# A graph network on one core: the two convolution passes take one-hots from memory and run their maxima on 32 rows, and the gated pass makes its angle on TensorE

## The chip, the cores and the metric

One core of a Trainium2 chip runs the whole program in one launch. The metric is the device time of that core in microseconds (us). Five engines take part: TensorE (PE; its weight loads are PEld), VectorE (DVE), ScalarE (ACT), GpSimd (POOL) and SyncE (SP), each with a sequencer of its own that issues its instructions in program order, waits for semaphores and does register work.

## The reference

Four graph layers run over 6,250 nodes with 128 features and 100,000 edges, each followed by a residual sum and a layer norm. The last layer is two transformer convolutions that share their edge features:

```python
    # L1: a gate per edge
    edge_weights = sigmoid(relu(ef @ We1 + be1) @ We2 + be2)[:, 0]
    aggr = segment_sum(edge_weights[:, None] * h_src, col, num_segments=n)
    # L3
    rel_t = last_update[src] - t
    rel_t_enc = jnp.cos(rel_t[:, None] * Wt[0][None, :] + bt)
    edge_attr = jnp.concatenate([rel_t_enc, msg], axis=-1)
    def transformer_conv(x, src, dst, edge_attr, ...):        # called twice, 4 heads of 32
        e = (edge_attr @ We).reshape(-1, HEADS, C)
        k_j = k[src] + e
        v_j = v[src] + e
        alpha = einsum('ehc,ehc->eh', q[dst], k_j) / sqrt(C)
        amax = segment_max(alpha, dst, num_segments=n)
        expa = exp(alpha - amax[dst])
        denom = segment_sum(expa, dst, num_segments=n)
        out = segment_sum(expa / denom[dst] * v_j, dst, num_segments=n)
        return out + x @ Wskip + bskip
```

## The kernel before

The edges are sorted by destination into 110 superblocks (turns) of 1,024 slots: eight tiles of 128 edges, in four groups of two tiles, each group with destinations of one bin of 128 nodes. A pass over the edges is a software pipeline of turns. There are seven: three relational attention passes, the gated pass (`gated_edges`), the attention pass of L2, and two convolution passes (`attention_edges` with `conv=1` and `conv=2`). The prediction speaks of the gated pass and of the two convolution passes.

The order on every engine is written out by hand in a function `step`. In a convolution pass `superblocks` calls it with three turns at once: `n` is scored, `m` gets its maxima and weights, `o` is summed. What happens to a turn:

- POOL gathers its 1,024 source rows with eight indirect DMAs (L970) into one of four buffers; it may start when the sums of the turn four back are done.
- DVE builds its one-hot, 128x1024, destination place by edge (`make_onehot`, L946). TensorE transposes it (L1087) and ACT copies it (L1203).
- TensorE spreads q of the destination with the flipped one-hot (L1109) and multiplies the edge features with We (L1112), in two halves of four tiles through one PSUM bank (`spread_half`). DVE adds e to k and v and multiplies with q (`convolve_half`, L1249 to L1251) and reduces to four scores per edge (`make_score`, L1288).
- Eight transposes bring the scores to 4 rows of 1,024 (`turn_scores`, L1122). Two scans of DVE run along them, up (L1258) and down (L1265), and give every edge the maximum of its segment, with the last turn's end carried in. Eight small transposes turn them back (`turn_top`, L1133), with the fall of the running maximum (L1272, L1135).
- DVE subtracts (L1279), ACT makes rate, factor and the exponentials (L1208, L1210, L1214), DVE weighs the rows (L1304), TensorE sums two tiles at a time with the one-hot (`sum_group`, L1147), and DVE adds each group's sum to its bin (`add_sums`, L1314).

Which bin a group has is read at run time: `load_bin` (L936) reads one number from SBUF into a register of the engine that asks, by the sequencer. TensorE and DVE read four a turn, ACT one. In `step` of DVE they stand in pairs behind the two scans; TensorE has its four between the third sum and the first half.

The gated pass works on turns `n` and `o`: one-hot, flip (L1452), copy (L1505), spread (L1467), dot product with the gate's weights (L1590 to L1597), sigmoid (L1517), weighing (L1545), sums (L1489, L1538). Beside it DVE makes the angle `rel*Wt+bt`, and takes whole turns off (L1561 to L1586, seven instructions, behind L1559 that makes `rel`); ACT takes the cosine (L1510), TensorE flips the features (L1478), ACT copies them (L1514), and SP stores them to DRAM (`edge_feat`) for the convolutions. DVE's four bin loads stand one by one between the instructions of the angle.

## Time and profile before

| what | us |
|---|---|
| median of 3 runs | 15725.96 (15695.67 to 15761.44) |
| profiled execution: span from first to last instruction | 13400.0 |
| gated pass, in the span | 6573 to 7999 |
| L2's attention pass | 8356 to 9512 |
| first convolution pass | 9796 to 11474 |
| second convolution pass | 11613 to 13303 |

The profiled execution's own time is not given beside its span. The timed runs are 2,326 us longer than the span, and no row shows what lies in that difference. Over the span DVE is busy for 78%, PE for 64%, POOL for 52% and ACT for 27%. A pass is read as 110 turns: a turn's time is the distance between two occurrences of an instruction that stands in it once.

### The profile page before, as it was taken

The page shows a single profiled execution, that of the slowest core. Times are in us where ns is not written, and L with a number is a line of the kernel's source. Part 1 is how long each engine was busy: PE and PEld are TensorE (multiplying, and loading weights), DVE is VectorE, ACT ScalarE, POOL GpSimd, SP SyncE. Part 2 cuts the span into 40 slices and gives each one's busy share as a digit, 9 for nine tenths or more (in the row PEclk, how much of TensorE's full clock was granted, in tenths as well). Part 3 has the DMA queues.
Part 4 walks back from the last instruction along what each step waited for, and adds up shares of the span by engine and source line. Part 5 has one row for each costly group of instructions (what it writes and reads, how often), then busy time and mean ns, then how long its engine had stood idle before and what let it go on. Part 6 is the DMA issues. An engine that isn't in the chain of part 4 may idle for free. (4 is left out here: it accounts for less than half of the span.)

```text
span 13400.0 us, 212567 instructions
## 1 busy us (share of the span) xinstructions
PE 8527.8 (64%) x52858; PEld 6962.8 (52%) x52859; DVE 10400.3 (78%) x15015; ACT 3614.6 (27%) x7819; POOL 6926.8 (52%) x7047
## 2 busy tenths in 40 slices
PE   4663477776777677775465652777266666567764
PEld 3553245554455535654455542555266666566664
DVE  8666569974799748996688875888778888688888
ACT  0111133332333233332244431333211111111111
POOL 2775047750477407772277750777145555255553
PEclk8555688877888788887688875666588888788887
DMA  4334754444544474443255550222233334233333
GB/s 182 113 113 119 244 206 106 106 80 193 192 106 106 72 292 123 106 106 53 79 145 145 146 111 19 55 55 54 19 103 106 107 107 105 75 108 105 105 106 72
DMA packets 720185, 1523.62 MB, mean 114 GB/s; under 512 B 364796, under 2 KB 416585, under 8 KB 680627
## 3 DMA queue, kind: packets, MB, share of 16 engines
q0 software_dynamic: 306624, 795.04, 25.0%
q1 hardware_dynamic: 413427, 727.07, 15.9%
q8 instruction: 51, 0.84, 0.0%
q14 instruction: 83, 0.68, 0.0%
HBM read 1050.48 MB, written 471.10 MB: 114 GB/s over the span
## 5 line engine op out<-in xcount | busy, mean ns | idle before, releaser
L970 POOL DMA_INDIRECT h<-table,edges_ring x3984 | 3856.5, 968 | 1889.0 <-issue 1154.3
L1147 PE MATMUL bank<-h,edges_onehot 128*128 128x260 f32 (+1 forms) x7968 | 1986.6, 406 | 652.3 <-issue 469.0
L1147 PEld LDWEIGHTS bank<-h,edges_onehot 128*128 128x128 f32 x7968 | 1570.6, 246 | 978.1 <-issue 717.4
L970 POOL DMA_INDIRECT edges_rows<-table,edges_ring x1512 | 1527.0, 1010 | 716.0 <-issue 431.0
L1122 PE MATMUL bank<-ident,edges_score 128*4 128x128 f32 x5280 | 1027.7, 360 | 1021.5 <-DVE edges_score L1288 737.9
L1258 DVE TENSOR_TENSOR_SCAN bank<-edges_fresh,edges_top,bank 4x1024 f32<-4x1024 bf16 x660 | 1541.5, 2336 | 144.9 <-PE bank L1122 141.2
L1265 DVE TENSOR_TENSOR_SCAN edges_top<-edges_fresh,bank 4x1024 f32<-4x1024 bf16 x660 | 1493.8, 2263 | 0.6 <-issue 0.3
L1122 PEld LDWEIGHTS bank<-ident,edges_score 128*4 128x4 f32 x5280 | 497.6, 104 | 1339.0 <-DVE edges_score L1288 784.9
L1314 DVE TENSOR_TENSOR acc<-acc,bank 128x260 f32 (+1 forms) x2640 | 908.9, 344 | 164.4 <-PE bank L1147 60.4
L2017 POOL DMA_INDIRECT rec<-dst,slots x782 | 797.0, 1019 | 432.7 <-issue 432.4
L1203 ACT ACTIVATE edges_onehotT<-bank 128x1024 bf16<-128x1024 bf16 (+1 forms) x550 | 562.1, 1022 | 1153.3 <-PE bank L1087 715.9
L970 POOL DMA_INDIRECT acc<-table,edges_ring x664 | 722.1, 1088 | 265.9 <-issue 199.8
L959 POOL COPY edges_ring<-rel_idx 128x64 uint32 (+2 forms) x42 | 10.3, 246 | 1575.5 <-POOLq L150 1575.4
L1191 ACT ACTIVATE edges_narrow_onehot<-edges_onehot 128x1024 bf16<-128x1024 f32 x444 | 469.2, 1057 | 1088.4 <-DVE edges_onehot L946 1088.4
L959 POOL COPY edges_ring<-src_idx 128x64 uint32 (+2 forms) x56 | 13.4, 239 | 1435.9 <-POOLq L150 1324.7
L1147 PE MATMUL bank<-edges_rows,edges_onehot 128*128 128x260 f32 (+1 forms) x2592 | 638.2, 401 | 169.3 <-issue 132.8
L1112 PE MATMUL bank<-edges_w_e,edge_score 128*128 128x128 f32 x3520 | 707.7, 284 | 0.0
L1208 ACT ACTIVATE edges_rate<-bank 128x4 f32<-128x4 f32 x660 | 114.4, 173 | 2168.8 <-PE bank L1135 2164.6
L1185 ACT ACTIVATE acc<-acc,edges_factor x2640 | 627.3, 309 | 92.3 <-issue 91.4
L1147 PEld LDWEIGHTS bank<-edges_rows,edges_onehot 128*128 128x128 f32 x2592 | 500.6, 240 | 281.4 <-issue 150.6
L1304 DVE TENSOR_TENSOR h<-h,bank 128x1024 f32<-128x1024 f32 x498 | 605.7, 1216 | 3.2 <-ACT bank L1214 1.1
L354 PE MATMUL bank<-source_w_rel,source_curT 128*128 128x512 f32 x1176 | 549.3, 612 | 88.5 <-DVE x L420 33.3
(346 smaller groups left out, 18152.3 us busy)
## 6 DMA issues: line engine op xcount, KB each, us to landing
table<-x SPq DMA_DIRECT2D x154, 1040.0 KB, 7.9
edge_score<-edge_feat SPq DMA_DIRECT2D x220, 512.0 KB, 3.8
table<-h SPq DMA_DIRECT2D x77, 1040.0 KB, 7.9
table<-source_typed_rows SPq DMA_DIRECT2D x63, 1040.0 KB, 8.1
h<-table,edges_ring POOLq DMA_INDIRECT x3984
edge_feat<-edge_score SPq DMA_DIRECT2D x110, 512.0 KB, 2.9
dst_row<-dst_rows SPq DMA_DIRECT2D x71, 704.0 KB, 4.2
buf<-rec SPq DMA_DIRECT2D x44, 840.0 KB, 5.2
```

What stands on the lines that cost most here:

```text
L354: ins = pe.matmul(g.bank[2 + half][:, q * 512:(q + 1) * 512], curT[:, j, :], w_rel[:, r:r + 4, :].rearrange("p r c -> p (r c)"), start=Tru ...
L970: pool.indirect_dma_start(out=rows[s % R][:, j, :], out_offset=None, in_=table, in_offset=bass.IndirectOffsetOnAxis(ap=ring[:, s * ST + j: ...
L1112: ins = pe.matmul(flip_b[:, 512 + j * P:512 + (j + 1) * P], feat[:, s, tile * P:(tile + 1) * P], w_e[:, :], start=True, stop=True)
L1122: ins = pe.transpose(score_b[0:HEADS, j * P:(j + 1) * P], score[s][:, j, :], g.ident[:, :])
L1147: ins = pe.matmul(sum_b[k % 3], onehot[s][:, j, :], rows[s][:, j, A0:W], start=j == k * GT, stop=j == (k + 1) * GT - 1)
L1185: ins = act.activation(part, part, ACT.Copy, scale=factor[s][:, head:head + 1])
L1203: act.activation(flippedT[s][:, :, :].rearrange("p t c -> p (t c)"), narrow_b[:, :] if conv is None else flip_b[:, :], ACT.Copy).then_inc( ...
L1258: v.tensor_tensor_scan(score_b[0:HEADS, :], fresh[s][:, 0:SLOTS_SB], score_b[0:HEADS, :], top[1 - s][:, SLOTS_SB - 1:SLOTS_SB], ALU.add, A ...
L1265: v.tensor_tensor_scan(top[s][:, ::-1], fresh[s][:, SLOTS_SB:0:-1], score_b[0:HEADS, ::-1], -BIG, ALU.add, ALU.max).then_inc(top_made, 1)
L1304: v.tensor_tensor(zr, zr, weight_t.unsqueeze(3).to_broadcast([P, ST, HEADS, DH]), ALU.mult).then_inc(rows_weighted, 1)
L1314: v.tensor_tensor(part, part, sum_b[k % 3], ALU.add).then_inc(sums_taken, 1)
L2017: pool.indirect_dma_start(out=rec, out_offset=bass.IndirectOffsetOnAxis(ap=slots[s][0:n, j:j + 1], axis=0), in_=recs[s][0:n, j * REC:(j + ...
```

## The change

**Convolution passes.** A new function `conv_edges` takes the place of `attention_edges` for them.
- One-hot and flipped one-hot are no longer made: SP loads both, 512 KB each a turn, from DRAM, where the gated pass has stored them.
- The pipeline has four stages (`stages`, turns `p, n, m, o`): the halves of turn `p` are spread one turn before DVE takes them, and each half has a bank of its own.
- The scores are kept as 32 rows (head by tile) of 128. One transpose turns them. The maxima have two levels: `find_ends` reduces each row's open ends (two instructions, each with a second that writes the 32x1 result), `line_up` brings these 64 numbers into one row on TensorE, `link` scans them (two scans of 32), `turn_line` turns them back, and `scan_both` runs two scans of 32x128 from there. The marks for it (`marks_d`, `lines_d`) are made once, before the passes.
- DVE's four bin loads stand together at the start of `step`, TensorE's between the second sum and `turn_line`. Sums are awaited in pairs.

**Gated pass.** The angle is one transpose of `rel` (9x128) and one product of 9x128 with a 9x512 table; DVE rounds it and subtracts (two instructions for seven). The flip of the one-hot runs a turn ahead, after the angle, and SP stores one-hot and flipped one-hot. The bin loads of DVE and of TensorE stand four in a row.

```diff
+def conv_edges(g, name, conv):
+                def load_features(p):
+                    hold(sp, half_ready, 2 * (u - 1))
+                    sp.dma_start(feat[s], g.edge_feat[:, bass.ds(u * (ST * P), ST * P)]).then_inc(feat_in[s], 16)
+                    sp.dma_start(onehotT[s], g.flip_d[:, bass.ds(u * (ST * P), ST * P)]).then_inc(feat_in[s], 16)
...
+                def step(p, n, m, o):          # TensorE
+                    if m:
+                        line_up(m)
+                    if o:
+                        sum_group(o, 0)
+                        sum_group(o, 1)
+                    if p:
+                        bins = load_bins(pe, g, number(p))
+                    if m:
+                        turn_line(m)
+                    if p:
+                        spread_half(p, 0, bins)
+                    if o:
+                        sum_group(o, 2)
+                        sum_group(o, 3)
+                    if m:
+                        turn_top(m)
+                    if p:
+                        spread_half(p, 1, bins)
+                    if n:
+                        turn_scores(n)
...
+                    act.activation(drop[:, :], drop_b, ACT.Relu).then_inc(drop_taken, 1)
+                    act.wait_ge(drop_taken, u + 1)
+                    act.activation(rate[s % 2][:, :], drop[:, :], ACT.Exp, scale=-1.0).then_inc(rate_made, 1)
...
+                def step(p, n, m, o):          # DVE
+                    bins = load_bins(v, g, number(o)) if o else []
+                    if m:
+                        find_ends(m)
+                    if n:
+                        convolve_half(n, 0)
+                    if o:
+                        add_sums(o, 0, bins)
+                        add_sums(o, 1, bins)
+                    if m:
+                        link(m)
+                    if n:
+                        convolve_half(n, 1)
+                    if m:
+                        scan_both(m)
+                    if n:
+                        make_score(n)
+                    if o:
+                        add_sums(o, 2, bins)
+                    if m:
+                        subtract_top(m)
+                    if o:
+                        add_sums(o, 3, bins)
+                    if m:
+                        weigh_rows(m)
...
+                def step(n, o, more=True):     # gated pass, TensorE
+                    if n:
+                        spread(n, load_bins(pe, g, number(n)))
+                    if o:
+                        sum_group(o, 0)
+                        sum_group(o, 1)
+                    if n:
+                        turn_rel(n)
+                    if o:
+                        flip_features(o)
+                    if n:
+                        make_angle(n)
+                    if n and more:
+                        flip_onehot(after(n))
+                    if o:
+                        sum_group(o, 2)
+                        sum_group(o, 3)
...
-        attention_edges(g, "edges31", table3, src_idx, conv=1)
+        conv_edges(g, "edges31", 1)
```

On DVE, in the first convolution pass: before, from the weighing of a turn's rows to the second scan.

```order
L1304 TENSOR_TENSOR edges_rows<-edges_rows,bank 128x8x4x32
L1257 ISA
L1258 SCALAR_TENSOR_TENSOR bank<-edges_fresh,edges_top,bank 4x1024
L936 ISA
L936 TENSOR_LOAD bin_row
L936 ISA x3
L936 TENSOR_LOAD bin_row
L936 ISA x2
L1314 ISA
L1314 TENSOR_TENSOR acc<-acc,bank 128x132
L95 REGISTER_ALU
L1265 SCALAR_TENSOR_TENSOR edges_top<-edges_fresh,bank 4x1024
```

The same place now: L1674 is the weighing, L940 the bin loads, the first row of L1617 the first instruction of `find_ends`.

```order
L1674 TENSOR_TENSOR edges_rows<-edges_rows,bank 128x8x4x32
L940 ISA
L940 TENSOR_LOAD bin_row
L940 ISA x3
L940 TENSOR_LOAD bin_row
L940 ISA x3
L940 TENSOR_LOAD bin_row
L940 ISA x3
L940 TENSOR_LOAD bin_row
L940 ISA x2
L1613 REGISTER_ALU
L1614 ISA
```

The long scans are gone from here, and all four loads stand behind the weighing; `find_ends` (L1617) follows the last row.

On TensorE, in the same pass: before, behind the eight score transposes.

```order
L1122 MATMUL bank<-ident,edges_score 4x128 x8
L1084 REGISTER_ALU
L95 REGISTER_ALU
L1087 MATMUL bank<-ident,edges_onehot 128x128 x8
L1147 MATMUL bank<-edges_rows,edges_onehot 128x132 x6
L936 ISA
L936 TENSOR_LOAD bin_row
```

And now, from the score transpose (L1505) over `line_up` (L1515) and two sums (L1546) to the loads; three more loads and `turn_line` (L1522, L1523) follow.

```order
L1505 MATMUL bank<-ident,edges_score 32x128
L1515 MATMUL bank<-pick,edges_ends 1x64 x2
L1515 MATMUL bank<-pick,edges_rising 1x64
L1546 MATMUL bank<-h,edges_onehot 128x132 x4
L940 TENSOR_LOAD bin_row
L940 ISA x2
```

Of the sixteen transposes that stood ahead of the loads one is left, and `line_up`, which waits for `find_ends` on DVE, stands in front.

On DVE in the gated pass: before, from the one-hot over the weighing (L1545) to the first instruction of the angle.

```order
L946 TENSOR_TENSOR edges_onehot<-place,places 128x1024
L1545 TENSOR_TENSOR acc<-acc,edges_gate 128x8x128
L936 ISA
L936 TENSOR_LOAD bin_row
L936 ISA x2
L1557 REGISTER_ALU
L1559 REGISTER_ALU
L1559 TENSOR_TENSOR edges_rel<-acc,rel_t 128x8
```

And now; L1975 is the weighing, two more loads and then L1981, the sum with the spread part, follow.

```order
L1969 REGISTER_ALU
L1969 TENSOR_TENSOR edges_rel<-acc,rel_t 128x8
L1975 TENSOR_TENSOR acc<-acc,edges_gate 128x8x128
L940 ISA
L940 TENSOR_LOAD bin_row
L940 ISA x3
L940 TENSOR_LOAD bin_row
L940 ISA x3
```

`rel` has moved ahead of the weighing, and the loads that stood between the angle's instructions stand together behind it.

## Rows read from the trace of the kernel before

**Rows 1.** Busy us by stretch (PE, PEld, DVE, ACT, POOL), clock, DMA share, GB/s.
```profile
6573.00:7999.00 1426.00, 849.99 (x5280) 778.58 (x5280) 1242.29 (x1872) 619.81 (x660) 990.84 (x894) 0.82 0.55 142
8356.00:9512.00 1156.00, 802.48 (x5500) 657.45 (x5500) 978.18 (x1547) 416.48 (x1103) 834.06 (x894) 0.67 0.30 53
9796.00:11474.00 1678.00, 1150.43 (x8140) 1045.66 (x8140) 1442.64 (x1877) 322.85 (x991) 898.63 (x894) 0.84 0.39 105
11613.00:13303.00 1690.00, 1167.08 (x8140) 1058.97 (x8140) 1442.52 (x1876) 322.85 (x991) 897.24 (x893) 0.82 0.39 104
```

**Rows 2.** Line L1288 in 9850:11450: count, ns min/median/max, first and last start.
```profile
L1288 DVE TENSOR_REDUCE edges_score<-h x79: 1219/1220/1220, 9878.3 to 11438.3; 128x32 f32<-128x1024 f32 x79
L1288 DVE TENSOR_REDUCE edges_score<-edges_rows x27: 1219/1220/1220, 9862.2 to 11423.0; 128x32 f32<-128x1024 f32 x27
```

**Rows 3.** DVE's timeline in a convolution turn: start, duration, then the instruction.
```profile
10500.01 0.29 DVE L1314 TENSOR_TENSOR acc<-acc,bank 128x132 f32 x1
10501.08 0.69 DVE L1249 TENSOR_TENSOR h<-h,bank 128x512 f32<-128x512 f32 x1 [0.79 <-PE bank L1112]
...
10503.13 1.22 DVE L1288 TENSOR_REDUCE edges_score<-h 128x32 f32<-128x1024 f32 x1
10504.26 1.21 DVE L1304 TENSOR_TENSOR h<-h,bank 128x1024 f32<-128x1024 f32 x1
10506.07 2.34 DVE L1258 TENSOR_TENSOR_SCAN bank<-edges_fresh,edges_top,bank 4x1024 f32<-4x1024 bf16 x1 [0.60 <-PE bank L1122]
...
10508.80 2.27 DVE L1265 TENSOR_TENSOR_SCAN edges_top<-edges_fresh,bank 4x1024 f32<-4x1024 bf16 x1
...
10513.60 1.22 DVE L946 TENSOR_TENSOR edges_onehot<-place,places 128x1024 f32<-128x1024 f32 x1
10514.74 0.18 DVE L1279 TENSOR_TENSOR edges_arg<-edges_score,bank 128x32 f32<-128x32 f32 x1
```

**Rows 4.** TensorE's timeline in the same turn and, last two rows, at the lower clock.
```profile
10504.40 1.52 PE L1122 MATMUL bank<-ident,edges_score 128*4 128x128 f32 x8 [3.35 <-DVE edges_score L1288]
...
10510.17 0.39 PE L1112 MATMUL bank<-edges_w_e,edge_score 128*128 128x128 f32 x2
10510.39 0.39 PE L1109 MATMUL bank<-dst,edge_score 128*128 x2
...
10511.28 0.62 PE L1147 MATMUL bank<-h,edges_onehot 128*128 128x132 f32 x4
...
10515.04 0.63 PE L1112 MATMUL bank<-edges_w_e,edge_score 128*128 128x128 f32 x2
...
10515.47 0.64 PE L1109 MATMUL bank<-dst,edge_score 128*128 x2
```

**Rows 5.** Line L936 in 10506:10509: count, ns min/median/max, first and last start.
```profile
L936 PEldq TENSOR_LOAD <-bin_row x4: 297/298/308, 10506.3 to 10508.5; - x4
```

**Rows 6.** ACT's timeline in the same turn.
```profile
10512.74 0.17 ACT L1208 ACTIVATE edges_rate<-bank 128x4 f32<-128x4 f32 x1 [3.98 <-PE bank L1135]
10513.06 0.39 ACT L1210 ACTIVATE edges_factor<-edges_rate,cold,hot 128x4 f32<-128x4 f32 x1
10514.95 0.20 ACT L1214 ACTIVATE bank<-edges_arg 128x32 f32<-128x32 f32 x1 [1.50 <-DVE edges_arg L1279]
```

**Rows 7.** Line L936 in 10506:10507.3, DVE's sequencer.
```profile
L936 DVEq TENSOR_LOAD <-bin_row x2: 305/310/316, 10506.2 to 10506.9; - x2
```

**Rows 8.** Line L1597 in 6600:7990, one a turn of the gated pass.
```profile
L1597 DVE TENSOR_REDUCE edges_dot<-acc x82: 1219/1220/1221, 6605.2 to 7983.7; 128x8 f32<-128x1024 f32 x82
L1597 DVE TENSOR_REDUCE edges_dot<-edges_rows x27: 1220/1220/1221, 6631.2 to 7958.5; 128x8 f32<-128x1024 f32 x27
```

**Rows 9.** The gathers in L2's pass (8400:9500): ns min/median/max.
```profile
L970 POOL DMA_INDIRECT h<-table,edges_ring x638: 940/944/992, 8399.3 to 9465.5; - x160
```

**Rows 10.** The page's GB/s in 40 slices of the span.
```profile
GB/s 182 113 113 119 244 206 106 106 80 193 192 106 106 72 292 123 106 106 53 79 145 145 146 111 19 55 55 54 19 103 106 107 107 105 75 108 105 105 106 72
```

**Rows 11.** DVE's timeline where the marks are made.
```profile
1476.02 1.23 DVE L2159 TENSOR_TENSOR new<-key,key_before 110x1024 f32<-110x1024 f32 x1 [12.88 <-DMA key_before<-key_d]
```

More of the change, by code:

```diff
@@ L46 @@
 SLOTS_SB = ST * P
+RUNS = HEADS * ST
+MARKS = 3 * P + 1
+LINE = 2 * RUNS
 RING = 4
@@ L54 @@
 TWO_PI = 6.283185307179586
+UNDER_TWO_PI = 6.2831845
 class Chain:
@@ L1364, in _, with back, stages, static @@
                 superblocks(v, step)
+def back(qs, by):
+    return (qs[0] + (qs[1] - by) // RING, (qs[1] - by) % RING)
+def stages(engine, step, depth):
+    def static(i):
+        at = [i - d for d in range(depth)]
+        step(*[(k // RING, k % RING) if 0 <= k < NSUPER else None for k in at])
+    for i in range(2 * RING):
+        static(i)
+    with engine.Fori(2, NSUPER // RING) as q:
+        for s in range(RING):
+            step(*[back((q, s), d) for d in range(depth)])
+    for i in range(NSUPER // RING * RING, NSUPER + depth - 1):
+        static(i)
@@ L1439, in _ @@
-                store(NSUPER // 2 - 1, 1)
+                store_onehot(0, 0)
+                full = (NSUPER - 2) // RING
+                for s in range(RING):
+                    turn((0, s), further(0, s, 1), further(0, s, 2))
+                with sp.Fori(1, full) as q:
+                    for s in range(RING):
+                        turn((q, s), further(q, s, 1), further(q, s, 2))
+                for s in range(NSUPER - full * RING):
+                    left = NSUPER - full * RING - s
+                    turn((full, s), further(full, s, 1) if left > 1 else None, further(full, s, 2) if left > 2 else None)
@@ new lines, in flip_onehot, with spread @@
+                def flip_onehot(n):
+                    u = number(n)
+                    pe.wait_ge(onehot_made, u + 1)
+                    hold(pe, flipped_kept, u)
+                    for j in range(ST):
+                        ins = pe.transpose(flip_b[:, j * P:(j + 1) * P], onehot[n[1]][:, j, :], g.ident[:, :])
+                    ins.then_inc(onehot_flipped, 1)
+                def spread(n, bins):
+                    u = number(n)
+                    pe.wait_ge(flipped_kept, u + 1)
+                    hold(pe, angle_made, u)
+                    for j in range(ST):
+                        ins = pe.matmul(dst_b[:, j * P:(j + 1) * P], flippedT[:, j, :],
+                                        g.dst[:, bass.ds(bins[j // GT], 1), :].rearrange("p b c -> p (b c)"),
+                                        start=True, stop=True)
+                    ins.then_inc(dst_spread, 1)
@@ L1598, in step @@
                     if o:
+                        take(o, 1, bins)
+                    if n and more:
+                        ahead(after(n))
+                    if n:
+                        v.wait_ge(angle_ready, u + 1)
+                        c.link(v.tensor_scalar(turns, angle_b, 12582912.0, 12582912.0, ALU.add, ALU.subtract))
+                        hold(v, cos_made, u)
+                        v.tensor_tensor(angle, angle_b, turns, ALU.subtract).then_inc(angle_made, 1)
+                    if o:
+                        take(o, 2, bins)
                         take(o, 3, bins)
                     if n:
-                        ahead(after(n))
                         c.end(L)
```

526 lines of the change are left out of this document (404 added, 122 removed).

## The prediction

> **What bounds the kernel now.** I read the stretches first, since the change touches three passes of seven [rows 1]: the convolutions take 1,678 and 1,690 us, the gated pass 1,426. Each is 110 turns. L1288 stands once in a turn of a convolution: from 9862.2 to 11438.3 there are 106 of them, 15.01 us a turn [rows 2]; with the second pass, longer by 12 us in 110 turns, the mean is 15.07. DVE is busy for 86% of the first convolution, POOL for 54%. DVE's timeline shows why [rows 3]: two scans of 2.34 and 2.27 us on 4 rows, a one-hot of 1.22, six instructions of 0.69 in the halves, a reduction of 1.22, a weighing of 1.21, four additions of 0.29. With the subtraction's 0.18 they add up to 13.7 us. So DVE's own work bounds the convolution before. The question is what bounds it when DVE's work is a third less; that is read from the order, the sequencers' rows and the waits between engines.
>
> **Convolution: what goes from DVE.** One-hot 1.22, the scans 4.61 and the fall's single column (priced as the subtraction, 0.18) go, 6.0 us. A scan's time follows the elements of a row: 2.3 us for 1,024, so 0.3 for 128 and 0.1 for 32, plus the fixed part, for which the smallest row here, 0.18 for 32 elements [rows 3], is the bound. I take 0.4 for each of the two scans of 32x128, with a handoff 0.9; 0.2 for each of 32, 0.4. `find_ends` has two passes over 32x128 and two 32x1 results that no row shows; between 0.4 (two of 0.18) and 1.6 (four of 0.4) I take 0.65, two additions of 132 columns. Starts in the timeline are a little closer than durations: a half is 2.05 us, the reduction 1.14, an addition 0.25. What DVE has left without the weighing is 2.05 + 0.5 + 0.4 + 2.05 + 0.9 + 1.14 + 0.65 (two additions, the subtraction) + 0.65 = 8.35 us, and 9.6 with it.
>
> **Convolution: the chain that replaces it.** The turn is now a ring of waits, and I add it up from the end of `find_ends` to the next one, at the higher clock.
> - TensorE's `line_up` waits for `find_ends`. Behind it stand four sums and then four bin loads. Before the loads 14 matmul instructions and their waits are issued: 28 took from 10504.4 [rows 4] to 10506.3 [rows 5], so 1.2 us for these, between 0.5 and 1.9. The loads start 0.75 us apart (10506.3 to 10508.5 for four), 3.0 us in all. That makes 4.2. Before, the same loads were hidden: the one-hot's flip and six sums were queued on the engine. Now the queue ahead is worth 1.6 us.
> - `turn_line`, the half of `p` and two sums stand between the loads and `turn_top`. A matmul instruction starts every 0.11 us (two between 10510.17 and 10510.39) [rows 4]; 4 + 16 + 8 + 5 of them are 3.7, with handoffs 4.0. Sum 8.2.
> - ACT then makes drop, rate, factor and weight: 0.17 twice, 0.39, 0.20 [rows 6] and gaps of 0.1 as between its rows, 1.35. Sum 9.55. DVE is through with its own part at 7.7 and waits here.
> - DVE issues the weighing, and its sequencer then reads four bins, 0.73 us apart (10506.2 to 10506.9) [rows 7], 2.9 and 0.2 of register work. The weighing covers 1.21 of this; before, each pair of loads stood behind a scan of 2.3 us, and nothing was seen of them. Sum 12.65, and `find_ends` 0.65: **13.3 us a turn** at the higher clock.
>
> **The clock.** At 1.2 GHz instructions start 0.21 us apart (two between 10515.04 and 10515.47) [rows 4], which adds 0.1 to each of 33 and some 0.5 in front of `link`: 3.8 us for a turn wholly there. The granted clock of the convolutions, 0.84 and 0.82 [rows 1], means a third of the time at the lower level (1 - 0.84 is half of 0.32). I keep 0.32: 13.3 + 1.2 = 14.5 us. Gain: 0.57 x 220 turns = **125 us**.
>
> **Gated pass.** L1597 from 6605.2 to 7983.7 is 109 turns, 12.76 us each [rows 8]. Five instructions on 512 columns fewer, at 0.69 at most as in a half [rows 3], take 3.1 to 3.4 us from DVE. What I find instead at the higher clock: weighing issued at 0.2, four loads until 3.7 (the first beside the weighing), sum, dot, one-hot and two bins' additions until 8.8, of which five instructions are of 1.2; the angle until 10.2; the last sums wait on TensorE for the flip, which waits for the one-hot (8.9): 8 and 8 instructions at 0.11 and handoffs, 11.1; the last addition 11.3. The other ring is TensorE's: its loads start when the last sums are issued, 9.9, end at 13.1, the spread takes 1.95, and DVE's sum starts at 15.1, which was 3.7 in its turn plus one period: 11.4 to **11.55 us**. At the lower clock the flip and two sums add 1.6. With a share of 0.36 (0.82 granted [rows 1]) 12.1 us, 0.65 x 110 = **70 us**.
>
> **Small things.** POOL is not late: its gathers take 0.944 us and start 1.25 us apart (638, three in four of all, from 8399.3 to 9465.5) [rows 9], 10.0 us for eight, and 10.1 with the copies of indices. DMA: a convolution turn moves 1.06 MB of rows and three times 0.52, 2.63 MB in 14.5 us or 181 GB/s, where a slice of this kernel reached 292 [rows 10]; each load is issued a turn ahead. The gated pass would have 240. The marks cost about eight passes over 110x1024, 1.23 us at most and 0.6 at least each [rows 11], and two scans of 2.3, with their stores (five, some 8 us to land): between 12 and 30 us, I take **20**, all exposed since no engine works beside it. Sum: 125 + 70 - 20 = 175 us.
>
> The profiled execution has a span of 13,400.0; it would be 13,225. The 2,326 us by which the timed runs are longer I carry over: 15,726 - 175 = **15,550 us**.
>
> **Rivals.**
> - *Shorter ring.* If TensorE issues more quickly, or the waits overlap, DVE's own row decides: 8.35 + 3.1 for the loads = 11.45 us, now with clock of no account. 3.62 x 220 = 796, with 70 and -20: 14,880. For it: DVE bounded before, and the two bins' loads are certain while 1.2 of issue is not. Against: five handoffs in a row.
> - *Gathers bound.* If the loads hide too, POOL's 10.1 is left, as in L2's pass (1,156 us [rows 1]), in the gated pass as well: 4.97 x 220 + 2.66 x 110 - 20 = 1,366 less, 14,360. Against: nothing on DVE stands between weighing and loads.
> - *Slower: the clock falls.* One ring with two waits of about 3 us on TensorE, in place of one of 3.4 [rows 4], and less work: L2's pass, whose matmuls are few, was granted 0.67 [rows 1], a share of 0.66 at 1.2 GHz. Then a convolution turn is 13.3 + 0.66 x 3.8 = 15.8, +160 us; the gated pass 12.6, -20; marks +20: 15,890. The sum turns positive at a share of about 0.5. The Trainium skill has this as its rule (TensorE: Matmul & The Clock Gate, Part 1): throttled is the default and activity releases it. By that rule fewer transposes and more waiting speak against the change; the trace agrees in L2's pass.
> - *The marks and waits cost what the engines save:* no change, within the forecast's upper part.
>
> **How the numbers follow.** The forecast has 0.52, with a range of its own of 13.6 to 15.0 us a convolution turn and 11.3 to 12.8 a gated one: 15,260 to 15,740. The shorter ring has 0.18, the fallen clock 0.2, the gathers 0.05, and 0.05 is for what I don't see. The range, 14,820 to 15,920, takes in most of the shorter ring and over half of the fallen clock and leaves out the gathers. What a measurement can tell from no change is 0.5%, 79 us: below 15,647 lie 0.42 of the forecast, the shorter ring and the gathers, 0.64; above 15,805 most of the fallen clock and some of the unseen, 0.2; between them 0.16.
>
> **What would show it.** DVE idle for about 1.7 us ahead of L1617 in each turn, with no releaser but issue, shows the loads; idle ahead of L1674 released by ACT shows the ring; PE's idle ahead of L1522 by issue shows TensorE's loads. POOL's waits for L1546 stay above 3 us a turn. If L1617 starts right behind L1674, the loads are hidden and I am wrong on the low side. If the granted clock of the convolutions is under 0.75, I am wrong on the high side. `find_ends` over 1.6 us, or gathers over 1.3 us, would break a term.

## The result, and the profile after

The changed kernel takes 16,360.18 us (median of 4 runs, 16,340.28 to 16,374.29) where the kernel before took 15,710.81 beside it (4 runs, 15,692.5 to 15,761.44). The ratio is 1.0413, with a 95% interval of 1.0391 to 1.0434: slower by 4.1%, some 650 us, where 15,550 us was forecast and the range ended at 15,920. The profiled execution took 16,359.05 us with a span of 16,357.1: nothing lies outside the span here.

The stretches of the two convolutions in the changed kernel answer to the last two rows of [rows 1]; the columns are the same.

```profile
11926.00:14024.00 2098.00, 1148.14 (x7040) 1049.94 (x7040) 976.98 (x2314) 221.40 (x991) 837.35 (x893) 0.68 0.46 140
14161.00:16262.00 2101.00, 1148.07 (x7040) 1050.29 (x7040) 977.12 (x2316) 221.41 (x991) 837.33 (x894) 0.68 0.47 140
```

DVE's work has fallen as planned, from 1,443 us to 977, 8.9 us a turn. The pass takes 2,098 us, and the clock is down from 0.84 to 0.68. What DVE waits for in the first of them (12000 to 13900; us in total, times, longest) names the place:

```profile
DVE acc L1684 <- remote: 490.7, 93, 6.0
DVE edges_masked L1617 <- issue: 192.7, 94, 2.5
DVE acc L1684 <- PE bank L1546: 185.3, 104, 2.4
DVE h L1674 <- ACT bank L1598: 43.6, 76, 0.6
```

The second row is the term for DVE's bin loads: 2.05 us ahead of `find_ends`, forecast at 1.7. The first is in no step of the forecast (L1684 adds a sum of TensorE to its bin). In 93 of 101 turns DVE waits 5.3 us for sums of TensorE, and "remote" means that the wait ended with a signal to which no instruction of the trace fits by its recorded end. The timeline of one turn shows it (start, duration, instruction, idle before and releaser; TensorE's weight loads left out):

```profile
13015.46 0.07 DVE L1617 DVE_READ_ACCUMULATOR2_ANT edges_ends<- 32x1 f32 x1
...
13015.67 0.57 PE L1515 MATMUL bank<-pick,edges_ends 32*1 32x64 f32 x4 [2.84 <-DVE edges_ends L1617]
13015.93 0.95 POOL L974 DMA_INDIRECT h<-table,edges_ring  x1 [0.30 <-issue]
...
13016.39 2.13 PE L1546 MATMUL bank<-edges_rows,edges_onehot 128*128 128x132 f32 x8
13016.65 0.67 DVE L1654 TENSOR_TENSOR h<-h,bank 128x512 f32<-128x512 f32 x1
...
13019.69 0.95 POOL L974 DMA_INDIRECT h<-table,edges_ring  x1 [0.30 <-issue]
13022.63 0.29 DVE L1684 TENSOR_TENSOR acc<-acc,bank 128x132 f32 x1 [5.31 <-remote]
...
13023.82 0.23 PE L1522 MATMUL bank<-ones,edges_linked 1*32 1x1 f32 x2 [5.30 <-DVE edges_linked L1626]
...
13025.38 0.47 DVE L1633 TENSOR_TENSOR_SCAN edges_rising<-edges_marks,bank 32x128 f32<-32x128 bf16 x1
```

The two sums are recorded as done at 13017.6 and 13018.5, and TensorE then does nothing but read its four bins. DVE, which waits for nothing but them, starts at 13022.6. The trace's list of semaphore updates has `line_up` (L1515) signalled at 13020.95 and the two sums at 13022.42 and 13022.48: 4.0 to 4.8 us late, and the last two 60 ns apart, although each sum takes 0.9 us. Meanwhile POOL issues the eight gathers of another turn. The last row is one of the new scans, 0.47 us where [rows 3] had 2.34: what was meant to get short did. The forecast's own sign for TensorE's loads, idle time ahead of L1522 (`turn_line`) that nothing but issue ends, is not there. The page of this profile puts that wait down to DVE's `link`, 1,171 us for the 220 turns of the two passes, 5.3 us a turn:

```profile
L1522 PE MATMUL bank<-ones,edges_linked 1*32 1x1 f32 x440 | 51.1, 183 | 1188.5 <-DVE edges_linked L1626 1171.4
```

### The profile page after: what moved, and what is told of

It reads as the page before. It is cut to its first block and busy times, and to the rows that moved or that the text cites. A ratio compares the mean times of both kernels' runs of the same rounds, so it can differ in the third digit from the quotient of the medians.

```text
span 16357.1 us, 210381 instructions
## 1 busy us (share of the span) xinstructions
PE 9344.6 (57%) x50988; PEld 7446.5 (46%) x50989; DVE 9217.8 (56%) x15380; ACT 3412.7 (21%) x7930; POOL 6767.2 (41%) x7047
## 5 line engine op out<-in xcount | busy, mean ns | idle before, releaser
L1151 PE MATMUL bank<-h,edges_onehot 128*128 128x260 f32 (+1 forms) x5312 | 1739.4, 492 | 1036.2 <-DVE acc L1318 724.5
L1151 PEld LDWEIGHTS bank<-h,edges_onehot 128*128 128x128 f32 x5312 | 1274.5, 274 | 1451.0 <-DVE acc L1318 762.7
L1262 DVE TENSOR_TENSOR_SCAN bank<-edges_fresh,edges_top,bank 4x1024 f32<-4x1024 bf16 x440 | 1028.9, 2338 | 605.8 <-remote 408.9
L1684 DVE TENSOR_TENSOR acc<-acc,bank 128x132 f32 x880 | 256.9, 292 | 1504.8 <-remote 1036.2
L1318 DVE TENSOR_TENSOR acc<-acc,bank 128x260 f32 (+1 forms) x1760 | 671.0, 381 | 760.7 <-remote 324.9
L1269 DVE TENSOR_TENSOR_SCAN edges_top<-edges_fresh,bank 4x1024 f32<-4x1024 bf16 x440 | 996.7, 2265 | 0.1
L1207 ACT ACTIVATE edges_onehotT<-bank 128x1024 bf16<-128x1024 bf16 x440 | 450.6, 1024 | 2027.3 <-remote 1974.2
L2370 PE MATMUL bank<-taken_before,edge_score 128*128 128x49 f32 x1564 | 348.7, 413 | 782.8 <-issue 772.0
L1496 PEld LDWEIGHTS bank<-edges_w_e,edge_score 128*128 128x128 f32 x3520 | 743.0, 261 | 0.0
L1522 PE MATMUL bank<-ones,edges_linked 1*32 1x1 f32 x440 | 51.1, 183 | 1188.5 <-DVE edges_linked L1626 1171.4
L2370 PEld LDWEIGHTS bank<-taken_before,edge_score 128*128 128x128 f32 x1564 | 339.1, 331 | 789.8 <-issue 789.8
```

What stands on the lines that cost most here:

```text
L1151: ins = pe.matmul(sum_b[k % 3], onehot[s][:, j, :], rows[s][:, j, A0:W], start=j == k * GT, stop=j == (k + 1) * GT - 1)
L1207: act.activation(flippedT[s][:, :, :].rearrange("p t c -> p (t c)"), narrow_b[:, :] if conv is None else flip_b[:, :], ACT.Copy).then_inc( ...
L1262: v.tensor_tensor_scan(score_b[0:HEADS, :], fresh[s][:, 0:SLOTS_SB], score_b[0:HEADS, :], top[1 - s][:, SLOTS_SB - 1:SLOTS_SB], ALU.add, A ...
L1269: v.tensor_tensor_scan(top[s][:, ::-1], fresh[s][:, SLOTS_SB:0:-1], score_b[0:HEADS, ::-1], -BIG, ALU.add, ALU.max).then_inc(top_made, 1)
L1318: v.tensor_tensor(part, part, sum_b[k % 3], ALU.add).then_inc(sums_taken, 1)
L1496: ins = pe.matmul(e_b[half][:, j * P:(j + 1) * P], feat[s][:, tile * P:(tile + 1) * P], w_e[:, :], start=True, stop=True)
```

## Is it the change or the profile that the forecast read?

The passes that the change leaves alone are some 400 us longer each than in the profile of before that stands above. So the kernel before was profiled once more.

> The kernel before, unchanged, profiled once more. The profile of the changed kernel has passes that the change leaves alone (three relational ones and L2's) which are some 400 us longer each than in the first profile of before. Theory A (the first profile was of a less disturbed execution than the timed runs): this span comes to 15,650 to 15,800 us, an unchanged pass takes 1,550 us and not 1,156, and a convolution turn is no longer 15.07 us but 17 to 19. Theory B (the change itself lengthens the passes that it does not touch): the span stays near 13,400 and the unchanged passes near 1,156.

Measured: 15,201.04 us with a span of 15,199.3 (this chip is some 3% faster than the first: 13 runs of before beside it have a median of 15,222.8). Theory A held in kind: the time lies inside the span. (The microseconds of the expectation are those of the first chip. A convolution turn comes to 16.1 us, 1,772 / 110, and not to 17 to 19.) The convolutions of before in this profile, again with the columns of [rows 1]:

```profile
11436.00:13208.00 1772.00, 1150.66 (x8140) 1044.55 (x8140) 1444.03 (x1877) 322.94 (x991) 886.17 (x893) 0.85 0.37 99
13345.00:15103.00 1758.00, 1149.91 (x8140) 1039.46 (x8140) 1444.51 (x1877) 322.91 (x991) 890.39 (x893) 0.85 0.37 100
```

A relational pass takes 1,492 us in place of 1,158, L2's pass 1,484 in place of 1,156, a convolution 1,772 in place of 1,678. What ACT waits for in the first relational pass, in the profile that the forecast read (1850 to 2950) and then in this one (2100 to 3450):

```profile
ACT edges_onehotT L1203 <- PE bank L1082: 129.7, 104, 3.3
```

```profile
ACT edges_onehotT L1203 <- remote: 393.2, 85, 6.4
```

It is the same signature as in the changed kernel, in code that the change does not touch. In the timeline of this pass:

```profile
2603.60 0.95 POOL L970 DMA_INDIRECT edges_rows<-table,edges_ring  x1 [0.30 <-issue]
...
2604.03 0.61 PE L1082 MATMUL bank<-identb,edges_narrow_onehot 128*128 128x128 bf16 x8
2606.52 0.42 DVE L1314 TENSOR_TENSOR acc<-acc,bank 128x260 f32 x1 [2.13 <-remote]
2606.56 1.02 ACT L1203 ACTIVATE edges_onehotT<-bank 128x1024 bf16<-128x1024 bf16 x1 [4.54 <-remote]
```

TensorE's flips end at 2604.6; three sums that ended between 2601.2 and 2604.2 are signalled at 2606.23, 2606.30 and 2606.36, the flips at 2606.46, and DVE and ACT start right behind. The landings of the last gather, which POOL had ended at 2604.5, are recorded from 2605.98 to 2606.36. So TensorE's signals arrive with the gather's. In the changed kernel this is the common case: of the late signals of its L1515 and L1546, 93% stand within 0.15 us of a recorded DMA update; of random instants 30% do.

The table counts signals of TensorE that stand over 1 us behind the recorded end of their matmul (over 8 us is left out, there the record itself is missing; where records are missing the next signal is taken, so a few of the late ones may be such gaps). The lines are the flips and sums of the first relational pass, or `line_up` and the sums of the first convolution; the turn is the mean distance of one instruction of DVE that stands in it once.

| kernel, pass | signals | late | mean of the late, us | turn, us |
|---|---|---|---|---|
| before, profile of the forecast, relational | 535 | 0 | - | 10.29 |
| before (e1), relational | 513 | 350 | 2.83 | 13.16 |
| changed, convolution | 507 | 271 | 4.46 | 18.79 |

In the convolutions of before only part of the turns is hit: of 104 turns in e1, 54 have no signal over 1 us late, and these take 15.01 us, the number of [rows 2]; the other 50 take 16.43.

Two things in these traces set a limit to every explanation that follows. The profile that the forecast read shows the same program with the same stream of gathers and no late signal, so the stream is not enough by itself. And in every execution with late signals records of landings are missing: a gather makes 16, and of the landings in the first convolution that profile has 16,363, e1 has 8,418. That the recording of so many landings is what holds the signals up is a rival which no run here settles, since every run was recorded.

## Which part, and where in the ring

> Changed gated pass with the convolutions of before; the marks are made but not used. Theory A (the loss of 650 us is in the convolutions): 15,640 to 15,760 us, the gated pass about even. Theory B (the gated pass with its 1 MB of stores a turn and its loads in a row is what got slower): 15,950 to 16,200.

```diff
-        conv_edges(g, "edges31", 1)
+        attention_edges(g, "edges31", g.table3, g.src_idx, conv=1)
```

Measured: 15,254.43 us, ratio 1.0019 (0.9997 to 1.004). The loss is in the convolutions. The marks put everything behind them 24 us later; the gated pass takes 1,552 us, in e1 1,523. So the gated pass is some 29 us slower, not 70 faster; that is one profile against one, and passes that are the same in both differ by up to 15 us.

> The changed kernel with TensorE's four bin loads of the convolutions moved to the start of step, ahead of line_up, where TensorE waits for DVE's ends anyway. Ring theory (the turn is a ring of waits, and the 3.0 us of TensorE's loads stand in it): 2 to 3 us a turn less, 220 turns, 15,700 to 15,900 us. Rival (TensorE is the bound in the slow turns, so that the loads cost the same anywhere): 16,250 to 16,360.

```diff
 def step(p, n, m, o):              # TensorE
+    if p:
+        bins = load_bins(pe, g, number(p))
     if m:
         line_up(m)
...
-    if p:
-        bins = load_bins(pe, g, number(p))
     if m:
         turn_line(m)
```

Measured: 15,880.95 us, ratio 1.0429 (1.0387 to 1.0471); the changed kernel had 1.0413. (That 15,881 lies in the ring theory's 15,700 to 15,900 is due to the faster chip; those bounds and those of e4 were set against a before of 15,711, so the ratio decides.) Three microseconds of loads out of the ring change nothing, a turn is still 18.64 us, and the signals of `line_up` and the sums are as late as before (281 of 510, 4.55 us). The ring theory missed by 2 us a turn.

> The changed kernel with DVE's four bin loads of the convolutions in two pairs, behind the first half and behind the score's reduction, in place of four in a row ahead of find_ends. Ring theory: find_ends comes 1.7 us sooner in a turn, some of which comes back behind the halves: 1 to 1.7 us a turn less, 15,980 to 16,140 us. Rival (DVE waits for TensorE anyway): 16,300 to 16,360.

```diff
-    bins = load_bins(v, g, number(o)) if o else []
+    bins = []
...
     if o:
+        bins += [load_bin(v, g, number(o), k) for k in (0, 1)]
         add_sums(o, 0, bins)
...
     if o:
+        bins += [load_bin(v, g, number(o), k) for k in (2, 3)]
         add_sums(o, 2, bins)
```

Measured: 15,782.26 us, ratio 1.0361 (1.0321 to 1.0402). About 0.5% less than the changed kernel, and 99 us less than e3 on the same chip, nearer to the rival than to the ring. The trace shows where the loads' time went. From the weighing to `find_ends` a turn takes 1.4 us in place of 3.3, as the ring theory has it; but from the end of `find_ends` to `turn_line`, where the late signals stand, it takes 9.2 us in place of 7.9 (means over some 100 turns).

> The changed kernel with the edits of the two runs before together: TensorE's bin loads at the start of step and DVE's in two pairs behind longer work. My ring of waits: 4 to 5 us a turn less, ratio to before 0.97 to 0.98. If the late signals of TensorE set the turn, the two edits add to no more than 1 us a turn: ratio 1.025 to 1.036.

The edits are those of e3 and e4.

Measured: 1.0395 (1.0365 to 1.0425). Together the moved loads give nothing that stands out from e4, and the ratio lies above both expected ranges. A ring out of which 4.7 us are moved and which does not get shorter ends its turn on something else, and the two stretches of e4 say on what: the time at which the signals come.

## What holds the signals

> The changed kernel, with two of the eight gathers a turn in the convolutions after the first four turns (the other six tiles keep what their rows held; the values are then of no use). In the traces of the timed condition TensorE's semaphore increments reach their waiters 2 to 5 us after the matmuls' recorded end, and at the moment at which a gather lands. Theory C (TensorE's increments are held up while gathers are in flight): line_up and the sums are signalled within 1 us, a convolution turn falls from 18.8 to 14 to 16 us, the kernel to 4% or more under the changed one (ratio to before 0.97 to 1.01). Rival D (the delay has nothing to do with the gathers, which take 10 us of a 19 us turn and bound nothing): ratio 1.035 to 1.045.

```diff
-        for j in range(ST):
+        for j in range(ST if few is None or (isinstance(u, int) and u < RING) else few):   # few=2
             pool.indirect_dma_start(...)
```

The cut leaves six of a turn's eight tiles without their rows, and the waits for landings count two in place of eight.

Measured: 15,053.13 us, ratio 0.9918 (0.9885 to 0.9951). Theory C held: against the changed kernel's 1.0413 it is 4.7% of the kernel. Not one of 531 signals is late, and the turn is 14.87 us. The place of the first timeline, in this kernel:

```profile
12505.28 0.07 DVE L1617 DVE_READ_ACCUMULATOR2_ANT edges_ends<- 32x1 f32 x1
...
12505.50 0.38 PE L1515 MATMUL bank<-pick,edges_ends 32*1 32x64 f32 x4 [2.87 <-DVE edges_ends L1617]
...
12505.92 1.23 PE L1546 MATMUL bank<-h,edges_onehot 128*128 128x132 f32 x8
12506.48 0.67 DVE L1654 TENSOR_TENSOR h<-h,bank 128x512 f32<-128x512 f32 x1
12507.31 0.29 DVE L1684 TENSOR_TENSOR acc<-acc,bank 128x132 f32 x1 [0.16 <-PE bank L1546]
...
12509.02 0.23 PE L1522 MATMUL bank<-ones,edges_linked 1*32 1x1 f32 x2 [1.87 <-DVE edges_linked L1626]
```

Where DVE had waited 5.31 us it waits 0.16. POOL's own time is not the explanation: in the changed kernel it waits almost 9 us a turn for sums. What is shown is that the delay goes with the gathers; whether it is the gathers or the recording of their landings is not (in this first convolution hardly a record of a landing is missing).

The same marks in both traces show where the turn is shorter (means of 100 turns of the changed kernel and 104 of e5, us):

| from ... to | changed | e5 |
|---|---|---|
| end of `find_ends` to `turn_line` | 7.90 | 3.95 |
| `turn_line` to `turn_top` | 5.31 | 5.29 |
| `turn_top` to the weighing | 1.82 | 1.84 |
| weighing to `find_ends` (DVE's loads) | 3.28 | 3.27 |
| `find_ends` | 0.50 | 0.50 |
| the turn | 18.81 | 14.85 |

The whole difference stands in the one step that waits for `line_up` and the first two sums.

> The changed kernel, with the one-hots and the flipped one-hots of the convolutions loaded for the first two turns only, so that 1 MB a turn is not moved (wrong one-hots afterwards). Theory E (the added 1 MB of loads a turn holds up the gathers and TensorE's signals): turn 15 to 17 us, ratio to before 0.98 to 1.02. Theory C (gathers alone do it): under 0.7 us a turn, ratio 1.03 to 1.04.

```diff
-                    sp.dma_start(onehotT[s], g.flip_d[...]).then_inc(feat_in[s], 16)
+                    if isinstance(u, int) and u < 2:
+                        sp.dma_start(onehotT[s], g.flip_d[...]).then_inc(feat_in[s], 16)
...
+                    if not isinstance(u, int) or u > 1:
+                        return
                     sp.dma_start(onehot[s][:, :], g.onehot_d[...]).then_inc(onehot_in[s], 16)
```

After the first two turns no one-hot and no flipped one-hot is loaded.

Measured: 15,844.46 us, ratio 1.0439 (1.0409 to 1.047). The traffic falls from 140 to 87 GB/s, 261 of 530 signals are late all the same, and the turn is 18.47 us. The added megabyte a turn costs nothing; theory E fell.

> The kernel before with the gathers of every pass issued in pairs: POOL issues two, waits until both have landed, and issues the next two; nothing else is changed. Theory C (many gathers in flight hold up TensorE's signals): the delays of 2 to 4 us behind L1147 and L1082 in the relational passes and L2's go, these passes fall by 1 to 2.5 us a turn, and the kernel is 2 to 6% faster than before (ratio 0.94 to 0.98). Rival G (it is not how many are in flight but that any are; the waits only slow POOL down, which bounds these passes): no delay goes, 0.5 to 1.5 us a turn more, ratio 1.02 to 1.06.

```diff
         for j in range(ST):
+            if j % 2 == 0 and j:
+                pool.wait_ge(gathered[s % R], g.base[s % R] + 16 * (ST * (q * 4 + s // R) + j))
+                park(pool)
+            elif j == 0 and (not isinstance(u, int) or u > 0):
+                pool.wait_ge(gathered[(s - 1) % R],
+                             g.base[(s - 1) % R] + 16 * ST * (q * 4 + (s - 1) // R + 1))
+                park(pool)
             pool.indirect_dma_start(...)
```

> The changed kernel with the gathers of every pass issued in pairs, as in the run ahead. Theory C: line_up and the sums are signalled within 1 us, a convolution turn takes 15 to 16 us as it did with two gathers a turn, ratio to before 0.93 to 0.99. Rival G: the delays stay, a turn of 19 us, ratio 1.04 to 1.08.

> The changed kernel with every gather issued only when the one before it has landed. Theory C: no delays either; POOL needs 8 x 1.5 to 2.4 us a turn, which hides in a convolution turn of 15 us at the shorter landing but not in the relational passes; ratio between 0.95 and 1.03, convolution turns as with pairs or up to 1 us more. Rival G: delays as before, ratio over 1.05.

The last two have the same edit in the changed kernel, e11 with 1 for 2.

Measured: ratios 1.2762, 1.3102 and 1.7645 to a before of 15,720.22 us. For e9 and e10 neither side's range held, and both sides were half right; e11 lies over the rival's 1.05, but without the rival's delays (0 of 405). The signals come on time: in e9's relational pass none of 480 is late, in e10's convolution 20 of 502, and these 20 look like missing records (7.4 us in the mean). But POOL becomes the bound: a turn takes about 20 us in e9's relational passes. The timeline of POOL in e10:

```profile
16003.50 0.95 POOL L980 DMA_INDIRECT h<-table,edges_ring  x1 [5.00 <-DMA h<-table,edges_ring]
16004.75 0.94 POOL L980 DMA_INDIRECT h<-table,edges_ring  x1 [0.30 <-issue]
16008.29 0.95 POOL L980 DMA_INDIRECT h<-table,edges_ring  x1 [2.59 <-DMA h<-table,edges_ring]
```

An instruction of 0.95 us is followed 3.54 us after its start by the one that waits for its data. I had taken a landing at 1.5 to 2.4 us, from the first records of landings. The Trainium skill says this of a gather's record (Perfetto Trace Analysis, DMA Instruction — SWDGE (GPSIMD)): its end is the end of writing the descriptors, not of moving the data. The trace agrees: the gather of 16004.75 is recorded as done at 16005.70, and its landings from 16007.17 to 16007.52.

## How many gathers, and what the ring is without them

> The changed kernel with the gathers of the two convolutions alone in groups of four, each group issued when the last has landed. With pairs the second gather of a pair started 1.25 us behind the first, and the next pair 3.5 us behind the second, so four take 7.3 us and a turn's eight 14.6. Theory C with a threshold (a few gathers in flight do no harm): a turn of 15 to 16 us, ratio to before 0.99 to 1.01. If four in a row hold the signals up already: turn 18 to 19, ratio 1.03 to 1.05.

Measured: 15,648.83 us beside 15,785.13, ratio **0.9919** (0.9891 to 0.9947). The edit is that of e9 with 4 for 2, in the convolutions alone. 36 of 532 signals of `line_up` and the sums count as late, but with a mean of 6.5 us and no nearer to landings (39% within 0.15 us) than random instants (42%); they look like missing records. The turn is 15.41 us, and the kernel is faster than both, than before by 0.8% (0.5 to 1.1): the same work as the changed kernel, with two waits more a turn on POOL, is 4.7% faster than it. Signals of TensorE's score transposes, for which `find_ends` waits, are late in 86 of 107 turns (2.0 us), so four in a row do some harm. Records of landings are missing here as well (10,030 in the first convolution, for 880 gathers and 330 loads of 16 landings each), and the sums are on time: missing records do not make late sums by themselves. What POOL waits for, from 12010 to 13650, shows that it is the bound now: a turn has 7.6 us of gathers, 1.9 between them and 5.9 of waits for landings, 15.4 in all (two more such rows have 75.5 and 73.5):

```profile
POOL h L980 <- DMA h<-table,edges_ring: 391.1, 133, 6.9
POOL edges_rows L980 <- DMA h<-table,edges_ring: 86.7, 26, 6.6
```

> The changed kernel with at most two gathers in flight in the convolutions: gather j waits for gather j-2, by a semaphore each for even and odd tiles. From the pairs: 3.5 us from a gather's start to the start of the one that waits for it, so 1.77 us a gather, 14.2 us a turn. Theory C: signals on time, a turn of 14.9 to 15.6 us, ratio 0.985 to 1.01. Rival G (the number in flight is not it): 19 us, ratio 1.04.

```diff
...
+            t = s if j > 1 else s - 1
+            last = (gathered if j % 2 == 0 else odd)[t % R]
+            pool.wait_ge(last, ...)        # gather j waits for gather j-2
+            park(pool)
             pool.indirect_dma_start(...).then_inc(landed, 16)   # even: gathered, odd: odd
```

Measured: 1.0158 (1.0116 to 1.02), a turn of 17.10 us. The signals are mostly on time, and POOL needs 2.1 us a gather, not 1.77: it bounds the turn at 17. The ratio lies above the range expected for theory C and well under the rival's.

> As the run ahead, and the bin loads of TensorE and DVE moved as in the earlier runs. With the signals on time my ring of waits should be what is left: the loads are 3.0 and 1.7 us of it, so the turn falls to 11.5 to 13 us unless POOL's 14.2 us bounds it: then 14.2 to 14.8 us, ratio 0.975 to 0.995. If the moved loads give nothing, as they did with the delays, the ring was wrong: ratio as in the run ahead.

> As the run ahead, and the eight filling matmuls ahead of turn_line. If TensorE's clock is still part of the turn: granted clock 0.75 to 0.85 in the convolutions and 0.3 to 0.8 us a turn less, ratio 0.97 to 0.99. If POOL bounds the turn: no difference from the run ahead, within 0.3%. If the filling work stands in the ring: 1 us a turn more.

To e13 come the edits of e3 and e4, and in e15 that of e8 (below).

Measured: 1.0137 (1.0095 to 1.018) and 1.0143 (1.0091 to 1.0196). The moved loads give nothing, which the expectation had as a sign against the ring; but POOL bounds these turns at 17 us, so the runs can't tell. Behind such a bound neither the loads nor the clock count, though the filling matmuls raise the granted clock of the first convolution from 0.71 to 0.82.

> The changed kernel; in the convolutions POOL waits once a turn, ahead of the fifth gather, until the four before it have landed (the groups of four waited a second time, between turns), and the bin loads of TensorE and DVE are moved as before. POOL then needs 8 x 1.25 + 2.6 = 12.6 us a turn, against 15.3 measured with both waits. Ring of waits: with signals on time and the loads out of the ring 13 to 14.5 us a turn, ratio to before 0.96 to 0.985. If the delays come back without the second wait: 16 to 18 us, ratio 1.0 to 1.03. If the loads are worth nothing: 15 us, ratio 0.99.

Of e12's edit the first branch is left, and the edits of e3 and e4 are added.

Measured: 15,830.38 us, ratio 1.0063 (1.0047 to 1.008), a turn of 16.39 us. The delays came back without the second wait (102 of 523 signals, 2.87 us), and 57 of 105 score transposes are signalled late as well; DVE waits 268 us for them ahead of `find_ends` in these turns. What the loads cost in the ring these turns do not show: in 8 of 104, counted with those transposes, no signal was late, and they took 13.06 us, but cut at the weighing in place of the score's reduction it is 15 turns of 14.8.

> As the run ahead, with the one wait in the gathers of all seven passes. POOL then needs 12.6 us a turn in the relational passes and L2's, where the turns take 13.2 to 13.6 us with the delays. Theory C: these signals come on time too, a turn of 12.7 to 13.0 us, 150 to 350 us less than the run ahead in five passes. Rival: POOL is the bound there and every wait is added, 13.5 to 16 us a turn, up to 1,000 us more.

Measured: 15,706.15 us, ratio 0.9982 (0.9973 to 0.9992), 124 us less than e16. L2's pass falls from 1,553 to 1,492 us, a relational one from 1,551 to 1,524. The gated pass rises by 30. That is a little under the 150 to 350 expected.

## The clock by itself

> The changed kernel with eight more 128x128 matmuls of the identity a turn on TensorE, in place of idling, between its bin loads and turn_line, into PSUM that nothing reads. Theory F (TensorE signals late when it goes idle behind a short burst, and at once when more matmuls follow): line_up and the sums are signalled at their end, the turn falls by 2 to 4 us, ratio 0.98 to 1.01. Clock theory (the low granted clock, 0.68, is the loss): clock over 0.8, ratio 1.01 to 1.03. Theory C: signals as late as before, ratio 1.035 to 1.06.

```diff
     if m:
+        for _ in range(8):
+            pe.matmul(g.bank[2][:, 768:896], g.ident[:, :], g.ident[:, :], start=True, stop=True)
         turn_line(m)
```

Measured: 15,559.85 us, ratio 1.0252 (1.0222 to 1.0282): work without use makes the changed kernel 1.6% faster. The first convolution:

```profile
11488.00:13408.00 1920.00, 1362.94 (x8800) 1238.72 (x8800) 964.00 (x2310) 221.43 (x991) 835.43 (x894) 0.77 0.51 153
```

The clock goes from 0.68 to 0.77 (over 0.8 was expected), the turn from 18.8 to 17.10. The signals are as late as without (281 of 549, 4.28 us), so theory F fell: what they wait for is not more work on TensorE. The Trainium skill has activity release the clock (TensorE: Matmul & The Clock Gate, Part 1); the trace agrees.

> As e16, with eight filling matmuls a turn on TensorE ahead of turn_line. Clock theory: granted clock 0.8 or more in the convolutions, and since POOL leaves room now 0.3 to 1 us a turn less, ratio 0.01 under e16. If the filling work stands in the ring or POOL bounds: 0 to 1 us more, ratio 0 to 0.01 over e16.

Measured: 15,731.12 us, ratio 0.9994 (0.9982 to 1.0005), 0.7% under e16, with a clock of 0.82. That the fill lengthens TensorE's queue costs less than the clock gives back.

## Why the prediction was wrong, step by step

- **"The 2,326 us ... I carry over."** This is the step that failed first. They do not lie outside the span, as e1 shows (1.7 us do); they lie in the passes, as TensorE's signals that come late, and the profile that I read had none. I had the difference of 17% in front of me and treated it as a constant. A convolution pass of before took 1,678 us in that profile and 1,772 in e1's; by the distance of L1288, 15.0 and 15.7 us a turn.
- **The term that the sum lacked** is that lateness. It stands in the ring's first step, "Behind it stand four sums and then four bin loads ... 4.2": 7.9 us measured, and 3.95 where the signals are on time. The turn is 18.8 against 14.9 us. The change puts two awaited signals of TensorE in the middle of the ten microseconds in which POOL issues a turn's gathers, with nothing queued on DVE behind them. Before, DVE had two scans and a one-hot to go on with, and half of the turns lost nothing.
- **The ring's path was wrong in that step.** I had TensorE's loads end it. In e5 DVE ends it in 65 of 103 turns: a half, two additions and `link` end 3.65 us behind `find_ends` in the mean, the loads 3.5. The trace lets me estimate what TensorE's loads cost there: 0.15 us a turn, where my sum had 3.0. (The "four sums" ahead of them are two, of eight matmuls; the 14 instructions are counted rightly.)
- **The ring's size came out by luck.** The other steps in e5: to `turn_top` 5.3 us (forecast 4.0 at the higher clock), ACT's part 1.8 (1.35), DVE's loads 3.3 (3.1), `find_ends` 0.5 (0.65). The sum is 14.85 and the forecast was 14.5. But with e5's clock, a share of 0.55 at 1.2 GHz, my terms give 13.3 + 0.55 x 3.8 = 15.4: a ring priced too long and a clock taken too high made up for each other. The gain was not there even so: e5's first convolution takes 1,677 us, that of the profile that I read 1,678 (beside e5 the kernel before took 15,176 us, 3% less than on the first chip, and e5 has a quarter of the gathers, so this is a rough comparison).
- **The clock** was granted at 0.68, a share of 0.64 at 1.2 GHz; I kept 0.32. The rival for it said 0.66, and 15.8 us a turn. Without late signals the share is 0.55 (e5). So that rival had its sign and the clock right, and the size was short by the lateness. My own mark, under 0.75, was met. What I gave for it does not bear it out: L2's pass has 5,500 matmuls in 1,156 us at 0.67, but the gated pass has fewer, 5,280 in 1,426 us, at 0.82 [rows 1]. What lowers and raises the clock here is shown by the change itself and by e8.
- **DVE's and POOL's work**: forecast 9.6 us a turn for DVE, measured 8.9. The scans of 32x128 take 0.47 and 0.48 us (0.4 each forecast), the gathers 0.948 (0.944 in [rows 9]). Right, and of no use, since both wait.
- **TensorE's loads** start 0.76 us apart (four from 13016.04 to 13018.31), as in [rows 5].
- **Gated pass**: forecast 70 us less, measured 29 more (e2 against e1, one profile each). DVE's work fell by 3.0 us a turn (1,243 to 911 us), as forecast; the clock went from 0.80 to 0.74. By my own terms that makes 12.4 us a turn, and 14.1 is measured. Its late signals were not taken away by themselves, so the remaining 1.7 us are not settled.
- **The marks**: forecast 20 us, measured 24 (e2 against e1).
- **The loads on DMA**: forecast as hidden, and they are (e6).
- **The sum**: -125 for the convolutions became +628 (e3 against e2, 4,160 against 3,532 us for the two; on that chip the changed kernel itself has no profile, and e3 has its ratio), -70 became +29, +20 became +24. The range ended at 15,920, since its worst case was the fallen clock alone.

## What to carry to other kernels

Compare a profile's span with the timed runs before building on it; where they differ by more than a per cent or two, the missing time can sit in waits that this profile does not show, as it did here, and then it need not stay constant under a change. Trading an engine's work for a ring of short waits made the signalling count at full price here, and TensorE's clock fell as well; the kernel before lost less, with work queued behind its waits. Where a stream of gathers runs beside a ring, breaking it into groups that wait for their landing can be worth more than any change in the ring (e12), as long as POOL's time stays under the turn.

## What the runs showed of the hardware

- TensorE's signals stood 2 to 5 us behind the recorded end of their matmuls while POOL streamed indirect DMAs, and came together with the landings. Of the signals of `line_up` and the sums 53% were late with eight gathers in a row (271 of 507), and none or hardly any with two a turn, in pairs that wait for each other, or in groups of four, where those of the score transposes still were. The same stream of eight had no late signal in the profile that the forecast read (0 of 535). Signals of ACT were not seen late, and those of DVE only where records are missing. The bytes moved were of no influence (e6).
- The mechanism inside is not shown. The profile without late signals holds 159,217 semaphore updates, that of e1 76,806 for the same program; of the 82,411 that are missing, 78,048 are landings of DMAs. All timed runs were recorded, so whether an unrecorded execution has the delay is open.
- From a gather's start to the start of the one that waits for its landing it takes 3.5 us, of which its own record shows 0.95.
- Eight useless matmuls of 128x128 a turn raised the granted clock from 0.68 to 0.77 and took 1.7 us off an 18.8 us turn.
